# Graph attention layer: TensorE's group signals sent by a drain in place of an increment on the last matmul

## The reference

```
sent   = x[src] @ Ws + bs
e_att  = sent + edge_attr @ We + be
recv   = x[dst] @ Wr + br
logits = mish(e_att + recv) . attn_w + attn_b            # per edge and head
w      = exp(logits - segment_max(logits, dst)[dst])
w      = w / segment_sum(w, dst)[dst]
out    = segment_sum(w * e_att, dst)
result = layernorm(x + out)
```

## Time and profile before

| | us |
|---|---|
| median of 3 plain runs | 2175.18 |
| lowest, highest | 2175.09, 2179.09 |
| span of the profiled execution | 2661.8 |

### The profile page before, as it was taken

The page is one execution under the profiler, slowest core; times in us unless marked ns, Lnnn a source line. Parts: engine busy times, 40 slices in busy tenths (PEclk is TensorE's granted clock), DMA queues, the critical chain, the costliest instruction groups (busy, mean ns, idle before and its releaser), DMA issues.

```text
span 2661.8 us, 45397 instructions
## 1 busy us (share of the span) xinstructions
PE 1917.4 (72%) x13621; PEld 1789.2 (67%) x13621; DVE 1895.0 (71%) x3941; ACT 1927.7 (72%) x3126; POOL 1575.1 (59%) x1640
## 2 busy tenths in 40 slices
PE   5667777777776777776776777776777777776776
PEld 5567666766666776766666766666667676666665
DVE  2676777777777767776676777766777777677766
ACT  1777777777777777777777777777777777777774
POOL 2666656656666665666566656656666666556661
PEclk8888888888888887888888888878888888878877
DMA  6422322322232322232232232232223232223220
GB/s 191 130 77 80 105 83 78 112 79 77 81 111 77 97 96 77 77 113 79 76 112 79 78 105 86 78 100 90 78 93 99 79 98 95 77 86 104 79 79 17
DMA packets 106714, 240.18 MB, mean 90 GB/s; under 512 B 45800, under 2 KB 72546, under 8 KB 99658
## 3 DMA queue, kind: packets, MB, share of 16 engines
q1 hardware_dynamic: 53334, 132.54, 14.6%
q0 software_dynamic: 52224, 107.06, 14.1%
q10 hardware_dynamic: 1128, 0.25, 0.0%
HBM read 229.98 MB, written 9.74 MB: 90 GB/s over the span
## 4 chain that ended last, share of the span: by engine, by line
DVE 36%; PE 20%; another core or an unknown queue 18%; issue 17%; ACT 7%; DVEq 1%; DMA 1%; ACTq 0%; SPq 0%
PE ps_sum L827 7%; DVE Z L1122 6%; DVE tbuf L1138 6%; DVE tbuf L1129 6%; DVE Z L1205 5%; PE ps_z L815 4%; PE ps_z L816 4%; DVE onehot L1113 4%; DVE logit L1144 2%; PE ps_edgeT L793 2%; ACT tbuf L933 1%; ACT tbuf L930 1%; ACT tbuf L936 1%; ACT tbuf L923 1%
## 5 line engine op out<-in xcount | busy, mean ns | idle before, releaser
L717 POOL DMA_INDIRECT landing<-xs_table,src_i x1632 | 1574.2, 965 | 1034.1 <-issue 448.3
L815 PE MATMUL ps_z<-we_sb,edgeT 128*128 128x128 f32 x3264 | 767.2, 320 | 83.3 <-issue 82.4
L816 PE MATMUL ps_z<-xr_buf,onehotT 128*128 128x128 f32 x3264 | 751.9, 315 | 72.3 <-issue 71.5
L827 PE MATMUL ps_sum<-Z,onehot 128*128 128x132 f32 x3264 | 558.9, 321 | 204.7 <-DVE att L1224 95.2
L815 PEld LDWEIGHTS ps_z<-we_sb,edgeT 128*128 128x128 f32 x3264 | 613.0, 232 | 100.9 <-issue 97.3
L816 PEld LDWEIGHTS ps_z<-xr_buf,onehotT 128*128 128x128 f32 x3264 | 609.4, 231 | 83.1 <-issue 82.8
L827 PEld LDWEIGHTS ps_sum<-Z,onehot 128*128 128x128 f32 x3264 | 485.6, 224 | 223.8 <-issue 149.4
L1113 DVE TENSOR_TENSOR onehot<-iota_f,ps_dve 128x512 f32<-128x512 f32 x408 | 276.0, 677 | 432.5 <-remote 352.6
L923 ACT ACTIVATE tbuf<-Z,c_zmax 128x512 f32<-128x512 f32 x408 | 296.2, 726 | 165.7 <-DVE Z L1122 85.9
L907 ACT COPY edgeT<-ps_edgeT 128x512 f32<-128x512 f32 x408 | 235.3, 577 | 229.4 <-remote 179.9
L798 PE MATMUL ps_onehotT<-ident_half,onehot 128*128 128x128 bf16 x1632 | 176.6, 232 | 241.8 <-issue 103.8
(11 more groups left out here) (110 smaller groups left out, 1228.3 us busy)
## 6 DMA issues: line engine op xcount, KB each, us to landing
landing<-in_edge_attr_dram SPq DMA_DIRECT2D x51, 2048.0 KB
landing<-xs_table,src_i POOLq DMA_INDIRECT x1632
x_in<-in_x_dram SPq DMA_DIRECT2D x51, 64.0 KB
xr_in<-xr_table SPq DMA_DIRECT2D x51, 64.0 KB
out_dram<-y_out SPq DMA_DIRECT2D x51, 64.0 KB
xr_buf<-xr_table SPq DMA_DIRECT2D x50, 64.0 KB
xs_table<-onehot SPq DMA_DIRECT2D x2, 896.0 KB
xr_table<-landing SPq DMA_DIRECT2D x1, 1568.0 KB
```

Of the source, the lines that this page charges most:

```text
L717: nc.gpsimd.indirect_dma_start(gath[b][:, t, :], None, xs_dram, bass.IndirectOffsetOnAxis(ap=src_i[:, b, t:t + 1], axis=0))\
L815: nc.tensor.matmul(ps_z[q][:, j, :], edgeT[:, q, j, :], we_sb[:, :], start=True, stop=False)
L816: mm = nc.tensor.matmul(ps_z[q][:, j, :], onehotT[:, q, j, :], xr_buf[:, b, :], start=False, stop=True)
L827: mm = nc.tensor.matmul(ps_sum[:, 0:ZC], OHv[:, b, t, :], Zv[:, b, t, :], start=(t == 0), stop=(t == T - 1))
```

## The change

In `turn`, `products` and `sums`, the increment that rode on the last matmul of the group is taken off, and a `drain` instruction on TensorE with the same increment follows the matmuls. That makes four drains per group, 32 per window, 1632 in all. The general path, the start and the steps on maxima keep increments on matmuls. Waits, values waited for, buffers and the order of all matmuls are as before, on every engine.

```diff
--- before.py
+++ after.py
@@ -790,14 +790,14 @@
                     pe.wait_ge(edge_landed[b], k * 16 + 16)
                 wait(pe, edgeT_ready, at(w, g) - 2)
                 for j in range(n):
-                    tr = nc.tensor.transpose(ps_edgeT[g % 2][:, j, :], edge_buf[:, b, a + j, :], ident[:, :])
-                tr.then_inc(edgeT_ps, 1)
+                    nc.tensor.transpose(ps_edgeT[g % 2][:, j, :], edge_buf[:, b, a + j, :], ident[:, :])
+                pe.drain().then_inc(edgeT_ps, 1)
                 pe.wait_ge(onehot_ready, at(w, g))
                 wait(pe, onehotT_ready, at(w, g) - 1)
                 for j in range(n):
-                    tr = nc.tensor.transpose(ps_onehotT[:, j, :].bitcast(BF16)[:, 0:P],
-                                             halves(OHv[:, b, a + j, :]), ident_half[:, :])
-                tr.then_inc(onehotT_ps, 1)
+                    nc.tensor.transpose(ps_onehotT[:, j, :].bitcast(BF16)[:, 0:P],
+                                        halves(OHv[:, b, a + j, :]), ident_half[:, :])
+                pe.drain().then_inc(onehotT_ps, 1)
 
             def products(w, b, k, g):
 
@@ -813,9 +813,9 @@
                         pe.wait_ge(xr_landed[b], k * 16 + (16 if b else 0))
                 for j in range(n):
                     nc.tensor.matmul(ps_z[q][:, j, :], edgeT[:, q, j, :], we_sb[:, :], start=True, stop=False)
-                    mm = nc.tensor.matmul(ps_z[q][:, j, :], onehotT[:, q, j, :], xr_buf[:, b, :],
-                                          start=False, stop=True)
-                mm.then_inc(z_ps, 1)
+                    nc.tensor.matmul(ps_z[q][:, j, :], onehotT[:, q, j, :], xr_buf[:, b, :],
+                                     start=False, stop=True)
+                pe.drain().then_inc(z_ps, 1)
 
             def sums(w, b, g):
 
@@ -824,9 +824,9 @@
                     wait(pe, fin, (w - 1) * FIN + FIN_READ)
                 pe.wait_ge(msg_ready, at(w, g))
                 for t in range(a, a + n):
-                    mm = nc.tensor.matmul(ps_sum[:, 0:ZC], OHv[:, b, t, :], Zv[:, b, t, :],
-                                          start=(t == 0), stop=(t == T - 1))
-                mm.then_inc(sum_ready, 1)
+                    nc.tensor.matmul(ps_sum[:, 0:ZC], OHv[:, b, t, :], Zv[:, b, t, :],
+                                     start=(t == 0), stop=(t == T - 1))
+                pe.drain().then_inc(sum_ready, 1)
 
             def ends_to_row(w, b):
                 pe.wait_ge(seg, w * SEG + SEG_A)
```

## The result

The kernel with drains takes **2226.17 us** (median of 4 runs, 2225.16 to 2229.01) beside 2175.14 us (median of 4, 2171.33 to 2179.09) for the kernel before. The ratio is 1.0238 with a 95% interval of 1.0223 to 1.0252. It is slower by 51 us. The prediction was 2180, slower with a chance of 0.58, in a range of 2165 to 2260. So the sign is right and the range holds the time, but the likeliest case was not what happened: rival B, in which TensorE (PE) sets the pace, comes nearest to it.

The account below looks back on a forecast made before the run. GpSimd's gathers were taken to pace the kernel and cover most drain time; start 0.7, end 2.9, last handovers 0.5 and loop 1 added 5.1 us to the 2175 us median, giving 2180, range 2165 to 2260.

Parts of the forecast that it names:

- rival B: In the loop, PE becomes the pace above 0.39 us a drain: 2190 to 2265 us; chance 0.30.
- E: On PE throughout, gaps in its work lower its clock, making the kernel slower; chance 0.05.
- GpSimd paces the kernel before: In the loop of plain runs, GpSimd's gathers set the pace: 1.268 us each, 40.6 us a window.
- A cost of recording: PE's signals, late by microseconds in the first profile, come from recording; 487 us separate its span from the plain median.
- rival C: Drains bring PE's late signals in time, so the kernel gets faster: 2146 to 2170 us; chance 0.12.
- PE's work, 28.2 us a window: PE's matmul work in a window at full clock, leaving 12.4 of 40.6 us free.
- a drain, 0.36 us: Price on PE of each of 32 drains a window, between bounds 0.30 and 0.44; 11.5 us a window.
- GpSimd still paces, by 0.9 us: In the loop with drains, PE needs 39.7 of 40.6 us a window, so GpSimd keeps the pace by 2%.
- It fits: In the loop, the order of waits absorbs PE's lateness: a heaviest group puts it 1.1 us behind, one without sums returns 1.5.
- Start, + 0.7: Before GpSimd's 17th gather, the last turn drain and the products' own drain add 0.7 us.
- End, + 2.9 and + 0.5: After the last gather, eight groups' drains in the last sums add 2.9 us, handovers of the last groups 0.5.
- D: The drain does not hold PE's queue, or restarting is free; start and end pay 1 to 2 us: 2177; chance 0.08.

Follow-up runs that it names:

- second profile: Kernel before, unchanged, profiled again in a batch where it takes 2174.17 us; the first profile's span was 2661.8 us.
- drains_456: Changed kernel with drains only in slots 4, 5 and 6 of each window (11 of 32): 2750.98 us, beside 2655.53 for the kernel before.
- all_but_edge: Changed kernel with edgeT_ps back on the last edge transpose (24 drains): 3074.3 us where before takes 2655.53; repeated where before takes about 2173, 2185.34.
- all_but_z: Changed kernel with z_ps back on the last product (24 of 32 drains): 3165.92 us, ratio 1.1954, where the kernel before takes 2655.53.

## Why the prediction was right or wrong

The sign came true and the time lies in the range, but not by the sum. Its own case ended at 2185, and 0.35 of the 0.58 for slower belonged to the rivals B and E; the range reached to 2260 for B alone.

**GpSimd paces the kernel before: right.** The halved gathers show it, and in the second profile it is never held after the start: gathers of neighbouring groups are 1.25 us apart. The sizes were off, each by a little and against each other: a gather is 1.283 us in the mean and not 1.268, the 17th starts at 61.0 and not 73.6, the tail behind the last is 39.0 and not 52.8. I had taken start and tail from an execution in which PE's signals came late.

**"A cost of recording": wrong.** Timed runs of the kernel before take as long as that profile in one batch, and its second profile is as short as the plain runs of its own. It led me to the right bound, since I set the late signals aside and reckoned with clean durations, but for a wrong reason. It also gave rival C its only support; C fell. One of the signs of being wrong was that the remote waits of the earlier trace rows vanish. They do vanish in after, but equally in the second profile of before, so this says nothing on the drains.

**PE's work, 28.2 us a window, and a drain, 0.36 us: right.** The passes of a window at their median distances in after make 27.5 us. A drain measured 0.374 in the mean, with the order that the working had: cheapest where a matmul follows at once (0.245, I had 0.30), dearer by 0.13 to 0.24 where a register or wait instruction stands behind the drain. In after, the next weight load starts 0.074 us (median) behind the modelled end of the last matmul where nothing stands behind the drain (L816 to L793), 0.20 behind it with one such instruction (0.198 with a wait, 0.206 with a register instruction) and 0.290 with one of each (L793 to L798). Before, such instructions did not show: L798 to L827, with a register instruction between in most of the 344 pairs, is 0.056 us, the distance of two one-hot transposes. The gap from L816 to L793, 0.356, is under the 0.4 to 0.55 that the prediction gave for it, and the one from L793 to L798, 0.594, is over the 0.5 that it named as a sign of being wrong. The step that "the sequencer issues nothing until the last matmul is complete", which no row of before shows, holds in after: behind none of the 1632 drains does an instruction of PE other than drains start before the modelled end of the last matmul, and no weight load sooner than 0.073 us behind it. In the second profile of before something starts during the last matmul at 1241 of the 1632 signals. The lower bound, 0.16 a drain with restarting free, was too low: the cheapest pair in the table has 0.245.

That the "four increments a group that ride on matmuls" are free holds too: with the increments back on the matmuls beside the drains the kernel takes 2227.43 us against 2226.17.

**"GpSimd still paces, by 0.9 us" and "It fits": the step that failed.** The sum gave 39.7 us of PE in a window; after has 27.5 + 12.0 = 39.5, so it was not the size of the drain. I compared PE's work with GpSimd's pace as if PE could fill its window to the last tenth. It can't. PE waits for ScalarE's copies and VectorE's one-hots and messages, and they wait for PE; at 42.04 us a window 2.5 us of PE are neither passes nor drains, of which 1.8 are waits on other engines (the 89 us below), and it was not pressed below that. The chain of waits of after shows the loop, here of the stretch from 1300 to 1345 us (start us, us, engine and line; "issue" is PE standing at a drain or at the instructions behind it):

```profile
1304.72 0.73 ACT tbuf L923
1305.48 0.73 ACT tbuf L930
1306.24 0.73 ACT tbuf L933
1306.99 0.73 ACT tbuf L936
...
1312.54 0.65 PE ps_edgeT L793 x4
1313.19 0.31 issue
1313.50 0.40 PE ps_onehotT L798 x4
1314.12 1.16 PE ps_sum L827 x8
...
1331.18 0.38 PE ps_ends L842 x2
1331.79 0.28 DVE ends_max L1179
```

From 1310.4 to 1331.6 PE is on the chain all along, with its stops at drains, and then the steps on maxima and ScalarE's passes take over until PE comes back. Neither PE (81% busy in matmuls) nor ScalarE (87%) is full, but PE's part has no room. By the line above the loss began at 0.26 us a drain and not at 0.39, and rival B's event came at 0.374, where its own formula would have given no loss. With the measured numbers the sum is (42.04 - 41.08) x 50 = 48, and the tail 2.7: 51.

**Why a window lengthens by only 0.27 of what PE stands** I can close roughly. PE's waits on other engines fell from 462 us (the five rows above) to 89 (all such rows of after), 7.5 us a window. The clock gave back the next part: it is recorded at two levels alone, 1.0 and 0.5, and at 0.5 for 371 us in the second profile of before (0.915 granted over the span) and for 46 us in after (0.99). At the low clock the 16 passes of a group's products are 0.21 apart (1313.91 to 1317.23, granted 0.52) in place of 0.11, so these 325 us are worth at most 160, 3.2 us a window. The window took 0.96. Together 11.7 of the 12.0. This is reckoned, not shown by a run.

**Start, + 0.7: measured + 0.3** (first to 17th gather 22.3 us before, 22.6 after). **End, + 2.9 and + 0.5: measured + 2.7.** It can be read in the last 64 passes of L827, of the second profile of before and of after:

```profile
2153.37 10.00 PE L827 MATMUL ps_sum<-Z,onehot 128*128 128x132 f32 x64 [4.53 <-DVE att L1224]
```

```profile
2203.88 11.74 PE L827 MATMUL ps_sum<-Z,onehot 128*128 128x132 f32 x64 [4.53 <-DVE att L1224]
```

Seven drains lie between eight groups, 1.74 / 7 = 0.25 us each, the price without exposed instructions, and not 0.36; "near 13" was too much.

**Rivals.** B is nearest to what occurred, but what paces is the loop and not a full PE: it begins from a lower point than I gave it and with a gentler slope, 0.27 in place of 1: 2215 at 0.41 in my sum, 2226 at 0.374 in fact. C fell: nothing became faster. Its drain "which empties PE before it signals" does so: in after the semaphore's update comes 0.034 us (median) behind the modelled end of the last matmul, against 0.014 for an increment on the matmul in the second profile of before. D fell with the gaps. E, to which I gave 0.05, was that gaps in PE's work lower its clock, with 0.50 granted behind a wait of 4.93 us and 0.99 in a busy stretch for it. It had the wrong sign, as below: the clock rose. What a lower clock costs here no run tells by itself.

## What to carry to other kernels

The room under a pace is not that engine's idle time: it ends where the loop of the other engines, each waiting for the next, becomes the longer one (38.84 us here, under a pace of 41.08), and one run with the pacing engine's work halved measures that loop. A drain on TensorE cost a quarter of a microsecond by itself here (0.245 us, L816 to L793) and then uncovered the sequencer instructions behind it (0.12 to 0.13 us for one, 0.22 for two), so a signal is better on the last matmul when work follows. Before reckoning with a profile, see that its span and the plain times can belong together; waits put down to "remote" and stops inside a group were the sign that they did not.

## What the runs showed of the hardware

**PE's clock rose with the gaps.** The granted clock of the same stretches, here of the second profile of before, to be read against the row of after above:

```profile
100.00:600.00 500.00, 390.91 (x3196) 369.92 (x3196) 444.87 (x918) 456.65 (x750) 381.28 (x390) 0.92 0.36 108
```

0.92 before, 0.99 after. In the second profile of before PE stood up to 4.5 us for the others and had 386 gaps of over 0.15 us from 65 us on, 233 of them over 1 us; in the first it came out of a wait of 4.93 us at a granted clock of 0.50. With the drains PE has 1176 gaps of over 0.15 us, 0.31 us in the median, and 8 of them are over 1 us. The stretches recorded at 0.5 went from 79 to 8. That the shorter gaps cause the higher clock is argued, not shown. With 21 and 24 drains the span's clock was 0.96. With half of the products left out it was 0.79 to 0.82, and the time at least 43 us above after. I had expected that gaps could only lower it.

**Passes, weight loads and waits on PE.** In the trace of before L815 and L816 have 3264 matmuls and 3264 weight loads each for 51 x 32 = 1632 fp32 products: two passes for one, each with its weight load. The transposes, fp32 (L793) and bf16 (L798), have 1632 of each, one for one. Of a group's waits it is not the last named one that the first weight load holds, as said ahead of the prediction: in after, the load of L815 carries the wait for `edgeT_ready` and that of L798 the wait for `onehot_ready`, the first named, in 384 of 408 groups each, and `onehotT_ready` and `z_ready` stand ahead of them as instructions of PE's sequencer. The reading of the earlier trace rows as a wait that the sequencer holds agrees with that.

**One program differs by 22% between two batches**: 2655.53 and about 2173 us for the kernel before. The record gives both batches the same chip number, 14, and they are six minutes apart, so it is not shown that two chips differ; the expectations above took it for that. The batch of 2655 us shows PE's signals arriving late by microseconds (ScalarE's cast starts 6.5 us behind the transposes in the earlier trace rows and 8.6 in drains_456), stops of PE in the middle of a group (318 of over 0.3 us) and a granted clock of 0.84 for the kernel before, against 0.92, and drains cost 0.17 to 0.42 us of time each in it instead of 0.03. With equal numbers of drains it also tells all_but_edge from all_but_z, by 92 us. Neither is explained by what I ran.
